# Addresses from packed steps, one register load a turn, and one-hots of two groups stored from GpSimd's queue

## What is computed

```python
src, dst = edge_index[0], edge_index[1]
gate = silu(edge_attr @ F1W + F1b) @ F2W + F2b
gate = gate + (emb[atom_z[src]] * (emb[atom_z[dst]] @ adapt)).sum(-1, keepdims=True)
msg = gate * h[dst] * (cw * mj)[:, None]
agg = segment_sum(msg, src)                       # also the sum of mj
h = _ln(h + agg / tot[:, None], gn, bn)
for i in range(4):                                # attention
    score = (Q[src] * K[dst]).sum(-1) + 0.1 * (edge_attr * Q[src][:, :40]).sum(-1) + logm[dst]
    es = exp(minimum(score - segment_max(score, src)[src], 20))
    aggi = segment_sum((es / denom[src])[:, None] * (h[dst] @ Wm[i]), src)
    h = _ln(h + leaky(concatenate([h, aggi]) @ Wu[i]), go[i], bo[i])
...
# L1, 5 steps, and L2, 10 steps: h = a * segment_sum(w[:, None] * h[row], col) + b * x
# L3: relu(einsum) by relation, a second einsum, then segment_sum over dst
```

## Time and profile before

| | |
|---|---|
| median of 3 runs | 10167.79 us (10154.54 to 10169.16) |
| the profiled execution | 10149.78 us |
| its span | 10148.0 us |
| TensorE busy, over the span | 7475.8 us (74%) |
| VectorE, GpSimd, ScalarE busy | 5440.0, 5066.9, 3421.9 us |
| mean granted clock of TensorE | 0.83 |
| data moved | 1702.10 MB |

### The profile page before, as it was taken

The page is one execution under the profiler, slowest core; times in us unless marked ns, Lnnn a source line. Parts: engine busy times, 40 slices in busy tenths (PEclk is TensorE's granted clock), DMA queues, the critical chain, the costliest instruction groups (busy, mean ns, idle before and its releaser), DMA issues. The chain is left out here.

```text
span 10148.0 us, 325152 instructions
## 1 busy us (share of the span) xinstructions
PE 7475.8 (74%) x108355; PEld 5850.9 (58%) x108356; DVE 5440.0 (54%) x18470; ACT 3421.9 (34%) x11841; POOL 5066.9 (50%) x6598
## 2 busy tenths in 40 slices
PE   1888865777777776996799499779958789973333
PEld 1555543555555565996699499669933344443333
DVE  7555555444444445998899799889941100012222
ACT  3222212444444443674477267447710000000000
POOL 0677773333333332553355155335537566747776
PEclk9999998666776777998899699889979999965555
DMA  8222222333333223995699299569948799931112
GB/s 327 56 62 62 62 60 93 129 128 135 134 123 136 97 87 99 258 263 139 191 265 264 68 260 263 140 189 263 264 169 321 303 372 368 356 120 21 21 21 20
DMA packets 1592522, 1702.10 MB, mean 168 GB/s; under 512 B 1260587, under 2 KB 1275323, under 8 KB 1546777
## 3 DMA queue, kind: packets, MB, share of 16 engines
q1 hardware_dynamic: 1234710, 1415.38, 44.1%
q10 hardware_dynamic: 252000, 210.40, 6.2%
q0 software_dynamic: 105248, 68.78, 3.7%
HBM read 1331.34 MB, written 361.02 MB: 167 GB/s over the span
## 5 line engine op out<-in xcount | busy, mean ns | idle before, releaser
L1778 POOL TENSOR_TENSOR m_passing<-m_passing 128x196 f32<-128x196 f32 x1488 | 762.5, 512 | 1825.2 <-ACT m_passing L1760 1747.1
L1204 PE MATMUL s_gotd<-m_table_d,s_hot 128*128 x17856 | 1365.1, 205 | 206.6 <-DMA s_hot<-OHT 195.5
L1760 ACT ACTIVATE m_passing<-s_gotd,s_es 128x49 f32<-128x49 f32 x5952 | 1304.4, 303 | 48.6 <-ACT s_es L1753 0.3
L1204 PE MATMUL s_gotq<-m_table_s,s_hot 128*128 x17856 | 1280.9, 185 | 5.6 <-issue 5.6
L1204 PEld LDWEIGHTS s_gotd<-m_table_d,s_hot 128*128 128x128 bf16 x17856 | 990.1, 96 | 289.3 <-DMA s_hot<-OHT 196.9
L1460 POOL TENSOR_TENSOR b_words<-b_words,b_rec 128x512 f32<-128x512 bf16 x372 | 389.5, 1047 | 1517.7 <-DVE b_words L1503 1517.7
L2045 POOL DMA_INDIRECT REC<-m_sums x800 | 956.7, 1196 | 352.1 <-issue 344.6
L483 POOL DMA_INDIRECT REC<-rec,place x800 | 964.1, 1205 | 260.7 <-issue 236.8
L1811 DVE TENSOR_REDUCE s_tops<-s_mt 128x512 f32 (+1 forms) x1488 | 1013.8, 681 | 3.7 <-PE s_mt L1721 3.6
L2078 PE MATMUL p_acc<-p_row,p_feats 128*64 128x512 f32 (+1 forms) x4032 | 902.2, 573 | 146.2 <-DMA p_row<-ADJ 145.4
L1204 PEld LDWEIGHTS s_gotq<-m_table_s,s_hot 128*128 128x128 bf16 x17856 | 992.9, 97 | 4.7 <-issue 4.7
(11 more groups left out here) (475 smaller groups left out, 17288.5 us busy)
## 6 DMA issues: line engine op xcount, KB each, us to landing
s_hot<-OHT SPq DMA_DIRECT2D x1488, 384.0 KB, 3.9
p_row<-ADJ SPq DMA_DIRECT2D x288, 1600.0 KB
s_rec<-REC SPq DMA_DIRECT2D x1488, 98.0 KB, 3.7
OHT<-b_turned ACTq DMA_DIRECT2D x372, 384.0 KB, 2.4
ADJ<-b_acc SPq DMA_DIRECT2D x25, 3200.0 KB, 11.5
REC<-fill SPq DMA_DIRECT2D x124, 624.0 KB, 8.8
b_rec<-REC ACTq DMA_DIRECT2D x372, 108.0 KB, 2.5
p_held<-ADJ ACTq DMA_DIRECT2D x14, 1600.0 KB, 34.4
```

What stands on the lines that cost most here:

```text
L1204: last = nc.tensor.matmul(out, hot, table[k][:, bass.ds(at, w)], start=(k == 0), stop=(k == 2))
L1760: last = nc.scalar.activation(msg[:, b % KEPT, j], gotd[b % KEPT][:, j, SW:2 * SW], ACT.Copy, scale=es[:, b % 2, j:j + 1])
L1778: nc.gpsimd.tensor_tensor(rest[:, b % KEPT].rearrange("p g w -> p (g w)"), msg[:, b % KEPT].rearrange("p g w -> p (g w)"), upper(msg[:, b ...
```

## The change

The tables change their layout. `where` has 8 numbers a group, four gather places and four `lands`, and one load brings them all. A `lands` number is the PSUM slot already multiplied to a column offset plus FIRST (2048) times the parts that were bits before; `leaves` has 8 numbers a group with bank and unit offsets and the sums place of the group three earlier.

In the build pass TensorE works out all addresses of a group's products in a new stage `landings`, and `addresses` moves ahead of `products`. `pe.to_reg(... * 4 + bank_at)` forms the register of exactly the address that a matmul will use. ScalarE does the same with one load. The store of `turned` goes from ScalarE's queue to GpSimd's, two groups at a time. VectorE writes a group's four one-hots in one operation.

```diff
-WHERE = G
+WHERE = 2 * G
+LEAVES = 8
+PSUM_AT = 1 << 25
...
-                laps(act, [(load, 0), (take_turned, LEAD), (store_turned, LEAD), (keep_sums, LEAD + 4),
-                           (move_out, LEAD + 1), (embeddings, LEAD + 1)], SLOTS)
+                laps(act, [(load, 0), (take_turned, LEAD), (ways_out, LEAD + 1),
+                           (keep_sums, LEAD + 4), (move_out, LEAD + 1), (embeddings, LEAD + 1)], SLOTS)
...
-                        at[b], lands[b] = load_places(nc, mem, n), load_lands(n)
+                        at[b] = load_places(nc, mem, n, 2 * G)
...
+                def landings(n, b, lap):
+                    slots, opens = [], []
+                    for j, x in enumerate(at[b][G:]):
+                        parts = x // FIRST
+                        slots.append(pe.snap(x - parts * FIRST).with_bounds(min_val=0, max_val=FIRST - 2 * P))
+                        if j == 0:
+                            fresh = pe.snap(parts // 16)
+                            parts = parts - fresh * 16
+                            opens.append(fresh.with_bounds(min_val=0, max_val=2 * AGG))
+                        opens.append(pe.snap(parts).with_bounds(min_val=0, max_val=2 * RING + 2))
+                        pe.to_reg(slots[j] * 4 + bank_at)
+                        pe.to_reg((slots[j] + P) * 4 + bank_at)
+                    for x in opens[0 if past(n, 3) else 1:]:
+                        pe.to_reg((x * (2 * P)) * 4 + bank_at)
+                    lands[b] = slots, opens
...
                 def products(n, b, lap):
                     pe.wait_ge(s_high, n + 1)
+                    slots, opens = lands[b]
                     for j in range(G):
-                        slot = pe.snap(lands[b][j] & 7).with_bounds(min_val=0, max_val=7)
-                        clear(pe.snap((lands[b][j] >> 3) & 15).with_bounds(min_val=0, max_val=2 * RING + 2))
+                        slot = slots[j]
+                        clear(opens[j - G])
...
-                laps(pe, [(own_offsets, 1), (turn, 0), (owned, 1), (add, 4), (products, 1), (addresses, 1),
+                laps(pe, [(own_offsets, 1), (turn, 0), (landings, 1), (owned, 1), (add, 4), (addresses, 1), (products, 1),
                           (gathers, 1), (offsets, 0)], SLOTS)
...
+                def store_turned(n, b, lap):
+                    if b % 2 == 0:
+                        return
+                    pool.wait_ge(s_turned, n + 1)
+                    pool.sem_inc(s_load, 1)
+                    first = (b - 1) % TURNED
+                    nc.gpsimd.dma_start(mem["OHT"][bass.ds(n - 1, 2)].rearrange("g p c -> p g c"),
+                                  turned[:, first:first + 2].rearrange("p n g k c -> p n (g k c)")
+                                  ).then_inc(s_oht[first // 2], 16)
...
-                laps(pool, [(high_words, 0), (less_high, LEAD), (less_middle, LEAD)], SLOTS)
+                laps(pool, [(high_words, 0), (store_turned, 3), (less_high, LEAD), (less_middle, LEAD)], SLOTS)
...
-                        dve.wait_ge(s_oht[b % TURNED], 16 * ((SLOTS // TURNED) * lap + b // TURNED))
-                    for j in range(G):
-                        v.tensor_scalar(turned[:, b % TURNED, j, 2], mem["iota_bf"][:],
-                                        rec[:, b, j, SL - CW:SL - CW + 1], None, ALU.is_equal)
+                        dve.wait_ge(s_oht[b % TURNED // 2], 16 * ((SLOTS // TURNED) * lap + b // TURNED))
+                    v.tensor_tensor(turned[:, b % TURNED, :, 2], mem["iota"][:].unsqueeze(1).to_broadcast([P, G, P]),
+                                    rec[:, b, :, SL - CW:SL - CW + 1].to_broadcast([P, G, P]), ALU.is_equal)
...
-        key = room.sb("key", [P, G, SW])
-        prod = room.sb("prod", [P, G, SW])
...
+        key, prod = (shared[:, used + k * G * SW:used + (k + 1) * G * SW].rearrange("p (g w) -> p g w", g=G)
+                     for k in range(2))
```

More of the change, by code:

```diff
@@ L675, in tile_tables @@
 def tile_tables(nc, mem):
-    for name, shape, dt in (("where", [1, NG * WHERE], I32), ("passing", [P, NG * 2 * G], I32),
+    for name, shape, dt in (("where", [1, NG * WHERE], I32), ("passing", [P, NG * LEAVES], I32),
                             ("spot", [1, T2], I32), ("goes_on", [P, NG], F32), ("fresh", [P, NG], F32),
                             ("last", [1, NB], I32), ("row_end", [1, NB], I32)):
+        if name == "passing":
+            mem["passing_at"] = -(-nc.sbuf_base // 32) * 32
         mem[name] = nc.alloc_sbuf_tensor("m_" + name, shape, dt)
-    mem["lands"], mem["leaves"] = (mem["passing"][0:1, k * NG * G:(k + 1) * NG * G] for k in range(2))
     with ExitStack() as ctx:
@@ L1260, in build_pass @@
         bank = room.ps("bank", [P, 8, 512])
+        bank_at = PSUM_AT
         flat = bank[:].rearrange("p b c -> p (b c)")
@@ L1330, in keep_sums @@
-                def keep_sums(n, b, lap):
-                    sums_place(n, b, lap)
-                    act.wait_ge(s_agg, n + 1)
-                    nc.scalar.copy(sums_flat[:, bass.ds(at["sums", b], SW)], agg).then_inc(s_part, 1)
+                        mem["passing"][0:1, bass.ds(n * LEAVES, LEAVES - 2)], engines=[act.engine], min_val=0,
+                        max_val=(DUMP + 1) * 2 * P, skip_runtime_bounds_check_because="tile_tables works them out")
+                    banks = [x.with_bounds(min_val=0, max_val=AGG * 512) for x in values[0:2]]
@@ L1335, in move_out, with keep_sums @@
+                    at[b] = banks, units, sums_at, kept
+                def keep_sums(n, b, lap):
+                    sums_at = (NB - 1) * SW if isinstance(n, int) and n + 3 >= NG else at[(b + 3) % SLOTS][2]
+                    act.wait_ge(s_agg, n + 1)
+                    act.sem_inc(s_load, 1)
+                    nc.scalar.copy(sums_flat[:, bass.ds(sums_at, SW)], agg).then_inc(s_part, 1)
                 def move_out(n, b, lap):
-                    ways_out(n, b, lap)
-                    banks, units, kept = at[b]
+                    banks, units, _, kept = at[b]
@@ L1405, in owned @@
                         pe.sem_inc(s_load, 1)
-                        clear(pe.snap(lands[b][0] >> 7).with_bounds(min_val=0, max_val=2 * AGG))
+                        clear(lands[b][1][0])
                 def add(n, b, lap):
```

91 lines of the change are left out of this document (44 added, 47 removed).

## The result

The changed kernel takes 10,185.75 us (median of 15 runs) where the kernel before takes 10,161.99 (15 runs). The ratio is 1.0024, with a 95% interval of 1.0016 to 1.0032: **a quarter of a per cent slower**. Forecast were 9,775 us, with a range of 9,480 to 10,080. The time lies outside it, and on the other side of no change. One of the 15 runs took 11,115 us at a mean granted clock of 0.65, where the others had 0.85 and 10,166 to 10,198; it is not in the ratio.

What follows compares the result with a forecast made beforehand. The prediction took TensorE's own instruction stream to bound the build pass. From 10150 us it took 480 for shorter build turns and added 104 for attention, giving 9775 us, range 9,480 to 10,080.

Steps and rivals of the forecast that it cites:

- The sum at the full clock: TensorE's build turn after the change: 4.17 us, with nine landings at 0.14 each, 0.6 of them hidden and 0.66 exposed.
- At the half level ... sum 4.40; all register work lies under it: TensorE's build turn at the 1.2 GHz clock: 1.36, 1.72 and 1.32 us, with register work hidden behind the matmuls.
- Both levels: TensorE's build turn: 4.4 us taken for full and half clock alike, from the half level; bounds 4.0 and 5.2.
- The lap branch: End of TensorE's unrolled build loop: body still fetched every lap, branch unchanged at 29 x 3.67 = 106 us.
- Rival (a): Build loop and attention: smaller body stays in the cache, lap branch falls and attention hides its operation: 9565 us; chance 0.2.
- Half stays: Build pass: of 0.2 us a turn left for other stalls, half remains, 0.1 us.
- The single load fits, no gap at the end: End of TensorE's build turn: the one load is hidden behind matmuls, removing the final gap of 0.42 to 0.5 us.
- GpSimd's store: Build pass: the 768 KB one-hot store lands in 3.6 to 4.8 us, hidden; its issue takes 587 ns.
- (b): Build pass: the store's landing bounds the turn; at 6.4 us the kernel takes 10,075, at 5.5 us 9,910; chance 0.18.
- (c): Build pass: GpSimd's store lands in 9 us or more, a turn takes 6.5 us, the kernel 10,590; chance 0.05.
- Attention: Attention passes: one more short TensorE register operation behind the wait for the tops, 0.07 us a turn, +104 us.
- Rival (d): Build pass: nine landings exposed ahead of the clear cost what 24 short operations did; turn near 5.2 us, 10,075; chance 0.07.

Runs made afterwards that it cites:

- e4_store: The kernel before with only the paired one-hot store on GpSimd's queue and a group's one-hots in one VectorE operation: 10,082.0 us, ratio 0.9922.
- e2_tops: The changed kernel with TensorE's address of the tops in the attention passes worked out ahead of the wait again: 10,050.68 us, ratio 0.989.
- e1_spread: The changed kernel with the landings of tiles 1 to 3 worked out inside the products, only tile 0's ahead of the clear: 9,803.13 us, ratio 0.9649.
- e10_two_loads: The changed kernel with two register loads of 4 numbers at the end of TensorE's turn instead of one of 8: 10,290.72 us, ratio 1.013.
- e5_six_spread: The changed kernel with TensorE's build loop of 6 turns, 3 word slots and landings of tiles 1 to 3 inside the products: 9,885.87 us, ratio 0.9732.
- e3_six: The changed kernel with TensorE's build loop unrolled 6 turns instead of 12 and 3 word slots instead of 4: 10,102.52 us, ratio 0.9937.
- e9_two_tiles: The changed kernel with landings of tiles 0 and 1 ahead of the first clear, those of tiles 2 and 3 inside the products: 9,859.18 us, ratio 0.9697.
- e8_spread_tops: The changed kernel with landings of tiles 1 to 3 inside the products and the tops' address ahead of the wait, 12 turns a lap: 9,678.4 us, ratio 0.9521.
- e6_before_six: The kernel before with TensorE's build loop unrolled 6 turns instead of 12 and 3 word slots instead of 4: 10,056.65 us, ratio 0.9895.

## Why the prediction was wrong

**What the chip said, in one account.** Before 10,162. The store and one-hots: -80 (e4_store, 10,082). The operation in the attention passes: +135 (e2_tops). What is left of the change, if the parts add up (e1_spread and e2_tops do, within 11 us), is the packed addresses and the merged loads on TensorE and ScalarE with their tables: 10,186 - 10,082 - 135 = **-31 us**, where the prediction had some -440 (480 less 37 for other stalls). Of these, TensorE's single load gives -105 (e10_two_loads). By difference the rest, the packed addresses above all, did not gain but cost some **+74 us**, of which the longer lap branch is 23 (29 times 0.79).

**TensorE's turn, the step that failed.** The sum at the full clock, 4.17 us, came near the 4.57 measured, in part by luck: the term of 0.66 us for the exposed landings measured 1.34, since I priced nine of them at the 0.14 of the gather addresses where they come at 0.19 each, with 0.4 hidden and not 0.6; clear, add and addresses took 0.80 instead of 1.07. The step that broke the forecast is "At the half level ... sum 4.40; all register work lies under it". The earlier trace rows did show the sequencer ahead, but at a place with one pair of short operations between matmuls. In the turns that lie wholly at the half level (medians, us, from one turn's first transpose to the next one's):

| | forecast | before, 65 turns | after, 29 turns |
|---|---|---|---|
| first transpose to the products' first clear | 1.36 | 1.37 | 2.80 |
| products, to the first gather | 1.72 | 2.80 | 1.80 |
| gathers, to the next transpose | 1.32 | 1.50 | 1.31 |
| turn | 4.40 | 5.69 | 5.94 |

Products and gathers came as forecast; the whole miss stands in the first row, where the landings take 1.22 us between the last transpose and the clear and the gather addresses another 0.3. The sequencer gets ahead only so far: in all 319 turns with a full record of the gathers, it ran the operation behind the last gather when 17 of the 24 gather matmuls were still to begin. In the turn above that is at 2603.09, 0.8 us before the last of them starts at the half level; then came the load of 0.59 us, and by the transposes nothing was left of the lead. Before, the 24 short operations had been spread between slow matmuls, where half-level products took 2.26 us from first to last start against 1.69 without them, so most of them was hidden; packing gathered them where nothing covers them. e1_spread undid this, with the same operations, and took 383 us, of which e5_six_spread against e3_six gives 217 to the block without the fetches.

**"Both levels" as one number.** I took 4.4 us at either clock and so never asked which share of time the clock would have. With the block the pass spent 1010 us at half level, with three operations 268. The trace of before had a row that asked for it: clock 0.69 in the build pass and 1.00 in the attention passes. It is shown that moving operations out of the block raised the clock, in e1_spread, e9_two_tiles and, without fetches, e5_six_spread. That less idle time as such raises it is not: the kernel before had TensorE busy for 302 of 400 us at 0.69, the changed one for 269 at 0.76, e1_spread for 306 at 0.90. What the chip decides by stays open. Nor did the change lose its gain by a fallen clock: the clock rose, and in e4_store, which has none of the packing, the time at the half level is 1081 us as against 1010.

**The lap branch** was left as it is, and that held nearly: 269 packets, branch 4.46 us instead of 3.67. The Trainium skill, "Advanced Engine Details and Errata", section ISA Cache, has 128 KB for TensorE; by that the bodies of 120 and 107 KB fit, and the trace of neither agrees. Rival (a) did not come. e1_spread has a body as long as that of the changed kernel (1708 instructions, begun 3 instructions later in the program), and most of its laps were not fetched; e8_spread_tops, with the same body at the same place, had more fetches (104 packets in 1640 to 3400 us). So at this size neither the size nor the place decides alone. With 856 instructions no lap is fetched (9 packets). Its price as an addend, 106 us, is borne out by e6_before_six (102, with the smaller ring).

**The other stalls.** "Half stays" was a guess, 37 us for the half that goes; e4_store gained 80, with the stall of ScalarE's body gone.

**The loads.** "The single load fits, no gap at the end": at the full clock an idle time of 0.28 us stayed before the transposes, since the load of 8 lasts 592 and not 333 ns; at the half level it is gone.

**GpSimd's store** landed in 4.1 us, inside the 3.6 to 4.8 taken; the wait for it was 54 us, nine times. The issue is 748 ns, not 587. Rivals (b) and (c) did not come. The prediction's estimate of 3.8 us rests on the Trainium skill, "DMA: Bandwidth & Descriptors", section "Anatomy of one DMA — SWDGE (gpsimd) path", which has about 2.0 us plus the bytes over 436 GB/s; the trace, with 4.1 us, agrees nearly.

**VectorE's one-hots** took 718 ns in the mean, nearly the 692 of the earlier trace rows, and nobody waited for them.

**Attention** was right: 0.07 a turn and 104 us forecast, 0.085 and 126 in the trace, 135 by e2_tops.

**Rival (d)**, that the landings cost exposed what the short operations did, was the nearest in its mechanism: its turn of 5.2 us at both levels is still short of the measured 5.9, and its time of 10,075 of the 10,186. It had a chance of 0.07.

## What to carry to other kernels

Register work on an engine's stream is not priced by its length but by what stands around it: six of the same packed operations showed no cost between the half-level matmuls of the products (1.68 us with them, 1.69 without), 0.45 us between those at the full clock, and nine in one block left a gap of 1.34 us in a turn of 5.8. Before an edit that gathers such work, look in the timeline for how far the sequencer is ahead at just that place, at each clock level, and take the clock's share of time as a term of its own. An unrolled body that is fetched at every lap shows in the instruction packets and in the time of its branch, and halving the unrolling may be worth more than thinning the body; an address that is worked out in another form than the matmul's costs an operation of its own, which matters behind a wait in a loop that TensorE fills.

## What the hardware showed that was not expected

- A fused register operation on TensorE lasts 46 to 205 ns; with what follows it, nine took 1.72 us, and the 24 short ones that they replace took 2.63 at the full clock, six in the 0.66 us of a tile, 0.11 each (the prediction had 0.07 at the least). 9 in place of 24 saved a third of the sequencer's time.
- TensorE's sequencer ran the operation behind the gathers at the same place in every turn, with 17 matmuls still to begin.
- A register load of 4 numbers takes 333 ns, one of 8 takes 592 (up to 1947), yet a second load in the turn cost 0.28 us.
- The granted clock of the build pass was 0.76 with 1.34 us of idle time in one block in each turn of some 5.8 us, 0.87 with 0.67 us, and 0.90 with 0.28 us.
- A loop body of 1708 instructions was fetched in every lap in one kernel (269 packets) and in a few laps in another (70). ScalarE's of 322 was fetched in every lap, one of 287 was not.
